# A four-layer graph network on one core: an earlier first chunk of scattered edges, a feature add on TensorE, reloaded counts on ACT's queue, and a new order in the perceptron

## What is computed

```python
h = jnp.maximum(_layernorm(x), 0.0); x = x + L0(h, src, dst)      # attention per edge over 4 heads
h = jnp.maximum(_layernorm(x), 0.0); x = x + L1(h, edge_index)    # two Chebyshev convolutions, K = 3
h = jnp.maximum(_layernorm(x), 0.0); x = x + L2(h, edge_attr_64)  # edge messages and a perceptron
h = jnp.maximum(_layernorm(x), 0.0); x = x + L3(h, src, dst)      # graph attention, softmax over edges

# L2, the layer that most of the change is about
message = jax.nn.relu(node_feats[edge_index[1]] + edge_feats)
message_reduce = jax.ops.segment_sum(message, edge_index[0], num_segments=num_nodes)
h = (1.0 + eps) * node_feats + message_reduce        # then W1, layernorm, relu, W2
```

## Time and profile before

| | us |
|---|---|
| median of 3 executions | 4118.89 |
| lowest, highest | 4100.37, 4125.41 |
| the profiled execution | 4078.07 |
| its span in the trace | 4076.3 |
| busy: PE, DVE | 1936.6, 2238.4 |
| busy: ACT, POOL | 1209.9, 1592.5 |
| mean granted clock of TensorE | 0.697 of full |

### The profile page before, as it was taken

One profiled execution on the slowest core, in us unless ns is written; L12 is line 12 of the kernel. 1 busy time (PEld: TensorE's weight loads), 2 busy tenths in 40 slices (PEclk: granted clock), 3 DMA queues, 4 the chain that ended last, 5 costly groups with the idle time before them and its releaser, 6 DMA issues. The chain is left out here.

```text
span 4076.3 us, 62411 instructions
## 1 busy us (share of the span) xinstructions
PE 1936.6 (48%) x16923; PEld 1342.4 (33%) x16923; DVE 2238.4 (55%) x4872; ACT 1209.9 (30%) x3818; POOL 1592.5 (39%) x1665
## 2 busy tenths in 40 slices
PE   5835544454444444330223249992211255655377
PEld 4623333333333333220111126661111245545222
DVE  6876766666676776430211013323211399997899
ACT  1154444444444444230001002100000133334744
POOL 0055555555555555456766640006667400000000
PEclk8966666666666666665555569995555598896599
DMA  8611111111111111542222210004443222221000
GB/s 277 249 42 40 40 40 40 40 40 40 40 40 40 40 40 40 172 124 55 59 52 53 52 34 1 0 11 138 136 115 102 61 75 83 74 82 42 0 0 8
DMA packets 399312, 266.91 MB, mean 65 GB/s; under 512 B 321473, under 2 KB 349310, under 8 KB 399090
## 3 DMA queue, kind: packets, MB, share of 16 engines
q1 hardware_dynamic: 306278, 87.81, 10.1%
q10 hardware_dynamic: 41488, 118.96, 8.1%
q0 software_dynamic: 51488, 59.40, 6.0%
HBM read 158.59 MB, written 107.47 MB: 65 GB/s over the span
## 5 line engine op out<-in xcount | busy, mean ns | idle before, releaser
L1229 POOL DMA_INDIRECT sorted_edges<-r_load,r_to x800 | 792.0, 990 | 736.3 <-DMA r_to<-places 439.6
L805 POOL DMA_INDIRECT hsrc<-h,edges x808 | 778.4, 963 | 693.5 <-PE ps L998 460.1
L873 DVE TENSOR_TENSOR prod<-ps,hsrc 125x1024 f32<-125x1024 f32 x200 | 245.0, 1225 | 323.3 <-remote 180.1
L996 PE MATMUL ps<-blank 128*64 128x160 bf16 x101 | 31.5, 312 | 590.2 <-remote 579.3
L1401 PE MATMUL ps<-R,w_work 128*128 128x64 bf16 x3000 | 145.1, 206 | 272.3 <-DVE R L1743 148.2
L1537 ACT ACTIVATE R<-w_work 128x384 bf16<-128x384 f32 (+1 forms) x160 | 85.8, 536 | 617.6 <-DVE w_work L1733 506.5
L1733 DVE TENSOR_TENSOR w_work<-ps,w_work 128x384 f32<-128x384 f32 (+1 forms) x160 | 91.2, 570 | 306.3 <-remote 296.6
L1391 PE MATMUL ps<-R 128*128 128x64 bf16 x3000 | 142.9, 208 | 225.5 <-issue 132.7
L1331 PE MATMUL ps<-R,A 128*128 128x192 bf16 x1250 | 183.0, 267 | 138.8 <-issue 136.0
L864 DVE TENSOR_SCALAR hot<-ramp,small 125x400 bf16<-125x400 int16 x800 | 219.6, 326 | 49.9 <-issue 47.7
L952 ACT ACTIVATE lo<-ramp,edges 125x128 bf16<-125x128 int16 x808 | 246.8, 387 | 0.0
(11 more groups left out here) (414 smaller groups left out, 4419.4 us busy)
## 6 DMA issues: line engine op xcount, KB each, us to landing
...
```

Source lines behind the costliest of these rows:

```text
L805: g.indirect_dma_start(out=hsrc[:, s, t, :], out_offset=None, in_=S.h0[:, :], in_offset=bass.IndirectOffsetOnAxis(ap=edges.bitcast(I32)[:, ...
L873: v.tensor_tensor(prod[0:TP, :].rearrange("p (t h f) -> p t h f", t=HT, h=H), S.ps[0:TP, hf * 1024:(hf + 1) * 1024].rearrange("p (t h f) - ...
L1229: g.indirect_dma_start(out=S.sorted, out_offset=bass.IndirectOffsetOnAxis(ap=to[:, hf, t:t + 1], axis=0), in_=load[:, hf, t, :], in_offset ...
```

## The change

- `bring_half` issues the places first and the pairs last.
- In `attend`, SP loads the first pair of items, then the first half of chunk 0, waits for the clearing of `S.sorted`, writes its tail, and goes on with the pairs; behind the last item it loads the second half and, as POOL frees them, the halves of chunk 1. POOL scatters chunk 0 behind its last gathers. The semaphores of the scatter move from `spread` to the program.
- In `attend`, DVE takes the maximum and subtracts it right behind the sums, ahead of `place`, and finishes softmax and `AO` ahead of adding counts and projection.
- In `spread`, the transposes of `hpT` and their adds move from ahead of the groups to behind the 42nd. `S.counts` has runs of 1280 bytes where it had 3200. SP's loop starts at chunk 1 and no longer waits for the propagations; ACT loads the counts back, one DMA behind each of the first twelve pairs of items, and one more.
- A step of an item: PE adds the edge features with one fp32 matmul by the identity, 384 or 448 columns, that opens the gather's bank; L1733 goes; ACT and DVE read the bank. The lowest part is taken at the start of the next step.
- In `mlp`, ACT writes the rows of the mask ahead of the sums of squares of the last normalization.

```diff
@@ -699,12 +699,12 @@
...
+    sp.dma_start(S.to[:, hf, :], S.pos[:, bass.ds(c * TC + hf * HALF, HALF)]).then_inc(S.landed[hf], 16)
     sp.dma_start(S.load[0:TP, hf, :, 0:D], I["edge_attr_64"][bass.ds(c * CE, CE), :].rearrange(by_edge, t=TC)[:, part, :]
                  ).then_inc(S.landed[hf], 16)
     with nc.allow_non_contiguous_dma(reason="two node numbers behind each row of features"):
         sp.dma_start(S.load[0:TP, hf, :, D:D + 2], S.pairs[bass.ds(c * CE, CE), :].rearrange(by_edge, t=TC)[:, part, :]
                      ).then_inc(S.landed[hf], 16)
-    sp.dma_start(S.to[:, hf, :], S.pos[:, bass.ds(c * TC + hf * HALF, HALF)]).then_inc(S.landed[hf], 16)
 
@@ -777,14 +778,22 @@
...
 
+            pair(0)
+            sp.wait_ge(S.padded, 1)
+            bring_half(nc, I, S, sp, 0, 0)
             sp.wait_ge(S.cleared, 16 * S.clears)
             r = sp.value_load(S.ovn[0:1, 2:3], min_val=0, max_val=E)
             sp.dma_start(S.sorted[bass.ds(r + OVB, P), :], S.zrow[0:ROW].unsqueeze(0).to_broadcast([P, ROW])).then_inc(S.tail, 16)
-            sp.wait_ge(S.padded, 1)
-            for hf in range(2):
-                bring_half(nc, I, S, sp, 0, hf)
+            with sp.Fori(1, n) as j:
+                pair(j)
+
             g, b = begin(n * 2, 0)
             line(g, n * 2)
+            bring_half(nc, I, S, sp, 0, 1)
+            for hf in range(2):
+                sp.wait_ge(S.sc[hf], 16 * HALF)
+                sp.sem_inc(S.ready, 1)
+                bring_half(nc, I, S, sp, 1, hf)
 
         @block.gpsimd
@@ -813,6 +822,13 @@
...
                     gather(i + 1, 1 - s, j * 16 + 16 + 16 * s)
+            g.wait_ge(S.tail, 16)
+            for hf in range(2):
+                g.wait_ge(S.landed[hf], 48)
+                g.sem_inc(q["carrier"], 1)
+                for t in range(HALF):
+                    g.indirect_dma_start(out=S.sorted, out_offset=bass.IndirectOffsetOnAxis(ap=S.to[:, hf, t:t + 1], axis=0),
+                                         in_=S.load[:, hf, t, :], in_offset=None).then_inc(S.sc[hf], 16)
@@ -902,21 +918,14 @@
                     else:
                         before = b0
                         own.step(v.tensor_copy(last[:, :], spot[0:1, s, 1:2]))
+                    own.settle(summed)
+                    v.wait_ge(q["summed"], 2 * i + 4)
+                    own.step(v.tensor_reduce(top, s4, AX.X, ALU.max))
+                    v.tensor_tensor(s4, s4, over(top, [TP, T, H]), ALU.subtract).then_inc(q["soft"], 1)
                     v.sem_inc(q["spot_free"], 1)
                     v.wait_ge(q["hot"], T * i + T)
                     v.sem_inc(q["edges_free"], 1)
                     place(own, i + 1, 1 - s, j * 16 + 16 + 16 * s)
-                    own.settle(summed)
-                    v.wait_ge(q["summed"], 2 * i + 4)
-                    topped = own.did(v.tensor_reduce(top, s4, AX.X, ALU.max))
-                    v.wait_ge(q["counted"], i + 1)
-                    add_counts(0)
-                    own.settle(topped)
-                    v.tensor_tensor(s4, s4, over(top, [TP, T, H]), ALU.subtract).then_inc(q["soft"], 1)
-                    add_counts(1)
-                    v.wait_ge(q["proj"], i + 2)
-                    v.tensor_tensor(S.hpw[:, bass.ds(before, W)], S.hpw[:, bass.ds(before, W)], S.ps[0:D, 3584:3584 + W],
-                                    ALU.add).then_inc(q["proj_free"], 1)
                     v.wait_ge(q["expo"], i + 1)
                     own.step(v.tensor_reduce(top, e4, AX.X, ALU.add))
                     own.step(v.reciprocal(top, top))
@@ -924,6 +933,12 @@
                     v.wait_ge(q["ao_free"], i + 2)
                     v.tensor_tensor(AO[0:TP, :, :, :], at[0:TP, :, :].unsqueeze(2).to_broadcast([TP, T, H, SUB]),
                                     a4.unsqueeze(3).to_broadcast([TP, T, H, SUB]), ALU.mult).then_inc(q["ao"], 1)
+                    v.wait_ge(q["counted"], i + 1)
+                    add_counts(0)
+                    add_counts(1)
+                    v.wait_ge(q["proj"], i + 2)
+                    v.tensor_tensor(S.hpw[:, bass.ds(before, W)], S.hpw[:, bass.ds(before, W)], S.ps[0:D, 3584:3584 + W],
+                                    ALU.add).then_inc(q["proj_free"], 1)
                     assert own.n == STEPS + s, (own.n, s)
@@ -1179,15 +1199,11 @@
...
                 for hf in range(2):
-                    sp.wait_ge(qr[f"sc{hf}"], c * (16 * HALF) + 16 * HALF)
-                    sp.sem_inc(qr["ready"], 1)
+                    sp.wait_ge(S.sc[hf], c * (16 * HALF) + 16 * HALF)
+                    sp.sem_inc(S.ready, 1)
                     bring_half(nc, I, S, sp, c + 1, hf)
 
-            def again(r):
-
-                sp.dma_start(counts[:, bass.ds(r, TAKE)], S.counts[bass.ds(r, TAKE)].rearrange("b k p n -> p b k n")).then_inc(q["again"], 16)
-
-            with sp.Fori(0, AFTER) as c:
+            with sp.Fori(1, AFTER) as c:
                 both(c)
@@ -1199,20 +1215,14 @@
...
-                again(c * TAKE)
-            with sp.Fori(AFTER + NB // TAKE, C2 - 1) as c:
+            with sp.Fori(AFTER, C2 - 1) as c:
                 both(c)
-            sp.dma_start(counts[:, NB - 1], S.counts[NB - 1].rearrange("k p n -> p k n")).then_inc(q["again"], 16)
             for hf in range(2):
-                sp.wait_ge(qr[f"sc{hf}"], C2 * 16 * HALF)
-                sp.sem_inc(qr["ready"], 1)
+                sp.wait_ge(S.sc[hf], C2 * 16 * HALF)
+                sp.sem_inc(S.ready, 1)
             with sp.Fori(0, rest_of(sp)) as k:
                 sp.wait_ge(qm["o_free"], k + 1)
@@ -1220,14 +1230,13 @@
...
-            g.wait_ge(S.tail, 16)
-            with g.Fori(0, C2) as c:
+            with g.Fori(1, C2) as c:
@@ -1242,16 +1251,20 @@
...
-            for b in range(NB):
-                if b % 8 == 0 and b >= 16:
-                    pe.wait_ge(q["hpt_free"], b // 8 - 1)
...
+                                      S.hpT[:, b * P:(b + 1) * P], S.ident[0:D, 0:D])
+                    if b % 8 == 7 or b == NB - 1:
+                        mm.then_inc(q["hpt"], 1)
+
             for n, (i, j, c) in enumerate(groups):
+                if n == MIDDLE:
+                    bring_sums()
                 if j == 0 and i % 5 == 0:
@@ -1362,10 +1375,16 @@
...
+            def features(n, s):
+
+                pe.matmul(S.bank[2 + n % 2][:, 0:size(n) * D], S.ident[:, :], es[:, s, cols_of(n), 0:D], start=True, stop=False,
+                          skip_group_check=True)
+
+            features(0, 0)
             for b in range(size(0)):
                 for d in range(SP3):
                     mm = pe.matmul(S.bank[2][:, b * D:(b + 1) * D], ohT[:, 0, b * P:(b + 1) * P], hw[:, 0, d, :],
-                                   start=(d == 0), stop=(d == SP3 - 1))
+                                   start=False, stop=(d == SP3 - 1), skip_group_check=True)
             mm.then_inc(qm["hg"], 1)
             with pe.Fori(0, pairs_of(pe)) as jj:
@@ -1386,16 +1405,18 @@
...
+                        features(n, s1)
                         for b in range(size(n)):
                             for d in range(SP3):
                                 mm = pe.matmul(S.bank[2 + k][:, b * D:(b + 1) * D],
-                                               ohT[:, k, b * P:(b + 1) * P], hw[:, s1, d, :], start=(d == 0), stop=(d == SP3 - 1))
+                                               ohT[:, k, b * P:(b + 1) * P], hw[:, s1, d, :], start=False, stop=(d == SP3 - 1),
+                                               skip_group_check=True)
                         mm.then_inc(qm["hg"], 1)
 
                     def scatter(n):
                         k = n % 2
                         pe.wait_ge(qm["lo"], i * GN + n + 1)
-                        pe.wait_ge(qm["low"], i * GN + n + 1)
+                        pe.wait_ge(qm["low"], i * GN + n + 2)
@@ -1519,22 +1540,28 @@
...
             n = pairs_of(act)
-            with act.Fori(0, n) as jj:
+            def again(r):
+
+                act.dma_start(counts[:, bass.ds(r, TAKE)], S.counts[bass.ds(r, TAKE)].rearrange("b k p n -> p b k n")).then_inc(q["again"], 16)
+
+            def pair(jj):
+
                 for s in range(2):
                     i = jj * 2 + s
                     for g in range(GN):
                         k, m = g % 2, size(g)
                         act.wait_ge(qm["sc"], i * GN + g + 1)
-                        act.wait_ge(qm["x"], i * GN + g + 1)
@@ -1542,6 +1569,14 @@
...
                             first = base_of(i + 2)
                     bring(i + 2, s, chunk, first)
+
+            with act.Fori(0, NB // TAKE) as jj:
+                pair(jj)
+                again(jj * TAKE)
+            act.dma_start(counts[:, NB - 1], S.counts[NB - 1].rearrange("k p n -> p k n")).then_inc(q["again"], 16)
+            with act.Fori(NB // TAKE, n) as jj:
+                pair(jj)
+            act.wait_ge(q["again"], 16 * (NB // TAKE + 1))
             for s in range(2):
```

(26 more changed lines are left out.)

58 lines of the change are left out of this document (32 added, 26 removed).

## The result

The kernel after took 4140.3 us (median of 7, 4131.2 to 4146.1) where the kernel before took 4116.4 (7, 4100.4 to 4125.4): a ratio of 1.0068, 95% interval 1.0043 to 1.0094. It is 24 us slower, and 30 us faster were forecast. The two profiled executions are further apart, 4146.1 and 4078.1, since that of before was 38 us under its median.

A forecast was written before the change was run, and what follows sets the result against it. No engine bounds it throughout; beside POOL's scatter the middle stage moves at 0.16 to 0.19 of free pace. Barrier to items' end 1947 for 2014 (-67), then +25 +16 +4 +0 -8: -30, so 4089 us on the median's scale, range 3980 to 4185.

The forecast's parts named there:

- Step 2: Barrier to block 8 of the first propagation: left at 725 us; spill's short runs 0, bounds 10 gained, 15 lost.
- Step 3: The scatter's hole goes: 15 chunks left, 434 us, in which propagations advance 69 us at 0.16 of free pace.
- Step 1: Layer 0 ends later, as chunk 0's 20 scatters run behind the last gathers: +25 us.
- Step 5: Items of the last message passing: 12.4 us each for 13.8, bounds 11.5 and 13.8; 40 items take 496 us.
- Rival C: Items bound by TensorE at a low clock (1.2 GHz): 15.4 us an item, +120, total 4209; chance 0.17.
- Step 6: Scatter's half chunks, with pairs landing last: a chunk up to 0.8 us longer, +16 us; bounds 0 and +31.
- Step 7: Counts brought back by ACT beside the first 24 items: +4 us, bounds 0 and +15.
- Step 9: Attention's 100 items, with DVE's new order: 0 us, bounds 0 and +40.
- rival B: Attention hangs on the scores, not the gathers: +0.4 us x 100 = +40, total 4129; chance 0.14.
- Step 10: Perceptron: squares now cover part of DVE's 14.1 us wait for rows, -8 us; bounds 0 and -14.
- Rival A: Propagations bear the scatter better, 0.35 of free pace for 0.16: 82 us more carried, total 4007; chance 0.26.
- Rival D: Middle stage: the crawl only moves from items to propagations, so the change does less; counted inside the sum, no own chance.

The follow-up runs named there:

- e3: Kernel after with runs of 3200 bytes in the spilled counts again; 2882.0 us, 0.9985 of before, on a chip where before takes 2886.0.
- h1: Kernel after with SP's wait for the end of the propagations put back ahead of chunk 24; 4176.4 us where before took 4117.2, one execution.
- h2: Kernel before with only the features on TensorE and the perceptron's rows ahead of its squares; 4065.1 us where before took 4117.2, one execution.
- f4: Kernel after without ACT's reload of the counts, so the last layer's mask is wrong; 2868.5 us where before took 2890.5, one execution.
- e2: Kernel after with DVE's order in the attention as before; 2898.8 us, 1.0062 of before, on a chip where before takes 2886.0.
- g1: Kernel before with the features on TensorE, the perceptron's rows first and DVE's new attention order; 2863.5 us, 0.9933 of before, where before takes 2882.0.

## Why the prediction was wrong, step by step

**Step 2 failed, and with it the sum.** "I leave this at 725 us": barrier to block 8 took 1146 (1740 to 2886). Of the 421 more, 214 lie in the groups and 220 in the first eight blocks (403 us for 183), and between them 12 were gained. The bound "15 us lost, if the spill ends later" had the right cause but was taken as its own price. ACT's copies in after, with the idle time ahead of them:

```profile
1762.25 0.27 ACT L1453 CAST A<-ps 128x128 bf16<-128x128 f32 x1 [24.22 <-issue]
...
1775.68 1.24 ACT L1453 CAST A<-ps 128x512 bf16<-128x512 f32 x3 [12.51 <-issue]
...
1787.66 1.46 ACT L1453 CAST A<-ps 128x512 bf16<-128x512 f32 x3 [9.34 <-issue]
```

ACT stood for 24.2, 12.5 and 9.3 us while it issued the spill of 16,000 short runs, and so 42 groups were done at the scatter's return where 59 were: 10 us late, by e3, which also shows that the short runs are what left them (61 for 42). Beside the scatter a group costs 11 us, not 0.6, so 17 groups more took some 190 us of scatter time that was then missing for blocks and items. What that is worth at the end is not 190 us but those times the pace of the work pushed out: by the forecast's own 0.16, 30 us, twice the bound. The term was mis-sized as I took a lateness at its free price ahead of a stretch that runs at a twentieth of that pace.

**Step 3 failed.** 0.16 of the free pace came from 8 blocks in 179 us. Two bursts, at 2302.6 and 2388.6, made 100 of their 200 matmuls, and the last block ran when the scatter had stopped. In after 7 blocks took 332 us from the first to the last, 55 each for 22 expected: 0.06 of the free pace. Over the last 16 chunks the mean was 0.12, and 0.14 in h1; but in after it also had to carry the stages that the groups had pushed back.

**What the two weigh.** The blocks began 542 us behind the barrier in before. So the forecast left 1175 - 542 = 633 us of scatter for them, which at 0.16 are 27 blocks; the trace had 399 us and 7 blocks. At 0.16 the 234 us fewer are 37 us of work, and 0.06 for 0.16 over the 399 is 39 more: together the 75 us by which the free propagations were longer. So the two errors weigh about the same. This split is worked out from traces and not run: no kernel with the long runs alone was timed where work crawls.

**Step 1** held: 24.3 us from the first to the twentieth scatter, and PE's last projection stood 31.5 us behind them. **Step 4**: 42 us for 30. **Step 5** held where nothing runs beside it: 12.4 us an item, the clock 0.99 to 1.00, and h2's 36 free items took (3698.8 - 3250.9 + 3.3) / 36 = 12.5. Rival C (the low clock) did not come. But the price of 1.91 ns a column was too low. The feature adds in after, window 3583 to 3783, two records a matmul:

```profile
L1380 PE MATMUL ps<-w_work,ident 128*128 128x384 f32 (+1 forms) x126 | 58.8, 548 | 0.0
```

63 matmuls of 400 columns on average in 58.8 us are 2.33 ns a column; h2 has the same (134.0 us for 144). PE was still busy for 9.6 us an item only (153.6 in 16) where step 5 added up 11.4, so that the item came out at its 12.4 by two errors against each other, which is luck in part. **Step 6** had the wrong sign: a chunk took 28.2 us for 28.9, since the pauses became shorter, and by the reading above, which is argued, that was the harm. **Step 7** was mis-sized: +4 with a bound of 15, measured 17 to 38 (f4) and 25 (24 items at 13.45 for 12.4). Before, the reload lay beside the scatter; what it cost there no run shows. **Step 8** held.

**Step 9** held: the attention was 21 us longer, but h2, with the old order, was as long. The lines of AO in h2 and in after:

```profile
L925 DVE TENSOR_TENSOR AO<-at,small x100: 691/691/710, 241.0 to 1706.5; 125x512 f32<-125x512 bf16 x100
```

```profile
L934 DVE TENSOR_TENSOR AO<-at,small x100: 691/692/719, 241.4 to 1703.8; 125x512 f32<-125x512 bf16 x100
```

1706.5 and 1703.8; the first profile of before, with 1682.8, was the odd one. With e2 and g1, where the order was worth nothing, rival B is out. **Step 10** held: DVE's wait for the rows fell from 14.1 to 2.8 us, and the end of the items to the end of the program from 369 to 362:

```profile
L2050 DVE SCALAR_TENSOR_TENSOR g_rows<-g_rows,Z 128x3200 f32<-128x3200 bf16 x25 | 88.8, 3551 | 4.6 <-ACT g_rows L1987 2.8
```

Rival A erred in direction: the pace was below 0.16, not above. Rival D named the right exchange and priced it at nothing.

The version that beats both is the kernel before with the features and the rows: 0.9930 of before (0.9899 to 0.9962) on one chip and 4065 for 4117, one execution each, on another.
